# Flagged head programs laid out behind the common one, and head norms as four matmuls side by side

## The chip, the cores and the metric

The kernel runs on one core of one Trainium2 chip. The metric is the device time of one launch in microseconds, taken from its start to its end on the chip. The kernel before took 3060.61 us, the median of 3 runs (3059.5 to 3063.14).

## The reference, cut to what matters

The input X has shape (4, 2048, 256). Four blocks are added to it in turn, each on a layer norm of what came before:

```
x = x + attention_a(layernorm(x))    # 16 heads of 16 channels, causal softmax(q k / 4) v, output projection
x = x + ffn(layernorm(x))            # shift by one token, sigmoid(xr W_r) * (relu(xk W_k)^2 W_v)
x = x + attention_b(layernorm(x))    # decayed keys of unit length times exp(10 key_scale), shifted queries,
                                     # mixed values of unit length, causal softmax, output projection
x = x + ffn(layernorm(x))            # the same feed-forward weights
```

Softmax in the kernel takes no row maximum where the scores of a head can't be large. Whether they can is found on the chip: a head is *flagged* when a bound on its scores is over 64. For attention A the bound is the largest query norm times the largest key norm of the head over all 2048 tokens of a batch, and for attention B the square of the key scale. In this case no head of A is flagged, and one head of the 16 of B is, for each of the four batches.

## The kernel before, in words

**Instances and slots.** The eight attentions (A and B of four batches, the list `ATT`) have four groups of four heads each, which makes 32 *instances*, n = 0 to 31. An instance is 68 *slots* of scores and products (`GROUPS`, `SETS`). For each slot TensorE makes scores with four 32-column tiles at once (`scores`, `matmul` at L863), ScalarE takes the exponential of 128x1024 of them (L819), GpSimd masks the diagonal (L722), and TensorE multiplies the probabilities with the values, four heads in four column tiles (`products`, L1070). Scores are made three slots ahead (`AHEAD`), in three pairs of PSUM banks; VectorE takes the sums out (`take`, L1430 and on).

**Jobs.** Projections, layer norms and feed-forward parts are *jobs* of 512 tokens, whose parts are put at slots by tables written by hand: `T_P` for the projections of attention A (kind P, 16 jobs), `T_M`, `T_B` and `T_END` for the rest. Each part takes one PSUM bank, whose place in the rotation is computed by `number_parts`. Each engine walks through the same slots and at each slot does its share of every job (`interleaved`, and on TensorE `slots`). P jobs of the first batch run ahead of instance 0; those of the second run in instances 0 to 3, and the others in 12, 13, 14, 15 and 16 to 19 at slots that follow the tables.

**Head norms.** A P job makes queries and keys for 512 tokens. VectorE squares their bf16 high parts (L1229), and TensorE sums the squares over the 16 channels of each head: two parts, `n0` for queries and `n1` for keys, each of two matmuls with 16 columns that add up in a 16x512 result (L918). VectorE takes the maximum of each part (`n_max`, L1234). After the fourth job of a batch VectorE takes the maximum of the four, multiplies queries' and keys' and compares (L1240 to L1244), TensorE turns the column of 16 flags to a row (the part `flag`, L925), and VectorE writes flags and the four group flags as integers (L1250 to L1255, semaphore `s_fl`).

**Branches on TensorE.** At the start of an instance TensorE loads the group's flag into a register (L1098) and branches (L1101). The stream of instructions holds the *plain* program of the instance, then its *flagged* program, then the `joined` block with the next load. The plain program first raises two semaphores for VectorE, whose flagged code waits on them (L1103 and the next line), runs its 68 slots, and jumps over the flagged program to `joined` (L1108); 12 slots ahead of the jump stands a prefetch hint (L1106). The flagged program goes through the four heads with a load and an If each (L1005, L1006); for a flagged head `row_maxima` makes all its scores once more in 40 matmuls and 16 for the mask (L990, L993), VectorE takes the maxima (L1388), TensorE turns them (L997), and SyncE places them by DMA in three rows of the queries (`place_maxima`, semaphore `placed`). Then come the 68 slots with the mask added by TensorE, and `joined` follows without a jump. The flagged instances here are 11, 15, 27 and 31, each with its fourth head (j = 3). VectorE and SyncE have Ifs of their own in their streams.

## Time and profile before

| | |
|---|---|
| median of 3 runs | 3060.61 us |
| the profiled execution's own time | 3063.15 us |
| its span, from the first to the last instruction | 3060.4 us |
| TensorE matmul busy | 2873.7 us (94%), 42980 matmuls |
| ScalarE busy | 2234.9 us (73%) |
| VectorE busy | 1482.4 us (48%) |
| GpSimd busy | 818.8 us (27%) |
| mean granted TensorE clock | 0.970 |

The profiled execution took 2.75 us more than its span. Busy time is the union of the spans of an engine's instructions; loads of weights are counted apart from matmuls. Branches, register loads and semaphore instructions are not counted as busy; a wait of an engine that ends with nothing that the profile shows to have released it is called "issue".

### The profile page before, as it was taken

The page shows a single profiled execution, that of the slowest core. Times are in us where ns is not written, and L with a number is a line of the kernel's source. Part 1 is how long each engine was busy: PE and PEld are TensorE (multiplying, and loading weights), DVE is VectorE, ACT ScalarE, POOL GpSimd, SP SyncE. Part 2 cuts the span into 40 slices and gives each one's busy share as a digit, 9 for nine tenths or more (in the row PEclk, how much of TensorE's full clock was granted, in tenths as well). Part 3 has the DMA queues.
Part 4 walks back from the last instruction along what each step waited for, and adds up shares of the span by engine and source line. Part 5 has one row for each costly group of instructions (what it writes and reads, how often), then busy time and mean ns, then how long its engine had stood idle before and what let it go on. Part 6 is the DMA issues. An engine that isn't in the chain of part 4 may idle for free.

```text
span 3060.4 us, 99660 instructions
## 1 busy us (share of the span) xinstructions
PE 2873.7 (94%) x42980; PEld 1286.8 (42%) x42980; DVE 1482.4 (48%) x3566; ACT 2234.9 (73%) x2487; POOL 818.8 (27%) x1246
## 2 busy tenths in 40 slices
PE   6999999999999799997999999999999979999697
PEld 3444444444444344443544444444444424444243
DVE  5322345565555664444344434555566555433344
ACT  2799877787787377883778877778778747888372
POOL 3222223333333222221222222333333312322011
PEclk9999999999999799997999999999999979999798
DMA  5332222222322123221322233222222211222111
GB/s 135 102 85 77 86 59 77 70 72 68 84 73 63 38 70 107 87 67 56 91 78 74 84 91 88 65 81 70 71 60 80 69 51 51 79 70 82 35 61 39
DMA packets 229839, 225.61 MB, mean 74 GB/s; under 512 B 33221, under 2 KB 212933, under 8 KB 229320
## 3 DMA queue, kind: packets, MB, share of 16 engines
q1 hardware_dynamic: 228504, 217.47, 25.0%
q8 instruction: 379, 6.21, 0.9%
q14 instruction: 140, 1.15, 0.1%
q10 hardware_dynamic: 816, 0.79, 0.1%
HBM read 146.80 MB, written 71.32 MB: 71 GB/s over the span
## 4 chain that ended last, share of the span: by engine, by line
PE 73%; DVE 15%; issue 7%; ACT 4%; POOL 1%; DMA 0%; SPq 0%; DVEq 0%; ACTq 0%
PE ps L863 46%; PE ps L1070 23%; ACT probs L819 3%; DVE pmax L1388 3%; PE ps L875 2%; DVE xn L1156 2%; DVE nw_y L1138 1%; DVE nw_u L1136 1%; DVE ln_st L1144 1%; DVE nw_u L1134 1%; DVE k_blk L1367 1%; DVE x_buf L1269 1%; DVE o_blk L1430 1%; DVE nw_v L1343 0%; POOL buf_k L694 0%
## 5 line engine op out<-in xcount | busy, mean ns | idle before, releaser
L819 ACT ACTIVATE probs<-ps 128x1024 f32<-128x1024 f32 x2176 | 2085.7, 1058 | 528.2 <-PE ps L863 525.0
L863 PE MATMUL ps<-q_st,k_st 99*32 99x256 bf16 (+3 forms) x20480 | 1247.8, 349 | 40.4 <-issue 20.8
L1070 PE MATMUL ps<-probs,v_st 128*17 128x512 f32 (+3 forms) x10240 | 1166.5, 532 | 15.5 <-POOL probs L722 9.0
L863 PEld LDWEIGHTS ps<-q_st,k_st 99*32 99x32 bf16 x20480 | 556.9, 96 | 815.7 <-issue 457.1
L722 POOL TENSOR_SCALAR_AFFINE_SELECT probs<-probs 128x256 f32<-128x256 f32 (+1 forms) x896 | 435.9, 503 | 1199.8 <-ACT probs L819 1187.8
L1070 PEld LDWEIGHTS ps<-probs,v_st 128*17 128x17 f32 x10240 | 290.1, 98 | 268.7 <-issue 57.8
L863 PE MATMUL ps<-xT,wT 128*32 128x512 f32 x2048 | 244.7, 594 | 0.0
L1430 DVE STREAM_TRANSPOSE o_blk<-ps 128x512 f32<-128x512 f32 x128 | 91.0, 711 | 273.3 <-PE ps L1070 273.0
L648 POOL TENSOR_TENSOR parts<-rest,parts 128x512 bf16<-128x512 f32 x96 | 120.9, 1259 | 318.3 <-DVE parts L1179 318.3
L1302 DVE SCALAR_TENSOR_TENSOR buf_v<-buf_v,ps 128x512 f32<-128x512 f32 x64 | 44.0, 688 | 273.1 <-PE ps L863 273.1
L1269 DVE TENSOR_TENSOR x_buf<-x_buf,ps 128x512 f32<-128x512 f32 x64 | 43.8, 685 | 235.3 <-PE ps L863 230.6
L863 PE MATMUL ps<-buf_k,wT 128*32 128x512 f32 x1024 | 125.3, 612 | 8.1 <-DVE buf_k L1289 8.1
L863 PE MATMUL ps<-wT,o_in 128*32 128x256 f32 x2048 | 127.3, 387 | 5.4 <-issue 5.2
L863 PEld LDWEIGHTS ps<-xT,wT 128*32 128x32 f32 x2048 | 66.4, 109 | 137.6 <-issue 133.4
L863 PE MATMUL ps<-wT,buf_u 128*32 128x256 f32 x2048 | 121.8, 379 | 1.6 <-issue 1.6
L863 PE MATMUL ps<-wT,buf_a 128*32 128x256 f32 x2048 | 121.5, 379 | 0.6 <-issue 0.5
L990 PE MATMUL ps<-k_st,q_st 99*128 99x512 bf16 (+3 forms) x160 | 66.7, 532 | 57.6 <-issue 51.3
L875 PE MATMUL ps<-ident,xn 128*128 128x128 f32 x512 | 85.0, 291 | 33.7 <-DVE xn L1156 19.7
L1174 DVE TENSOR_TENSOR rest<-ps,parts 128x512 f32<-128x512 f32 x64 | 44.2, 690 | 134.1 <-ACT parts L769 134.1
L783 ACT ACTIVATE buf_u<-ps 128x512 f32<-128x512 f32 x64 | 38.2, 597 | 96.8 <-PE ps L863 96.8
L875 PEld LDWEIGHTS ps<-ident,xn 128*128 128x128 f32 x512 | 55.1, 143 | 123.3 <-DVE xn L1156 63.3
L1388 DVE TENSOR_REDUCE pmax<-ps 128x1 f32<-128x1024 f32 (+4 forms) x96 | 80.4, 905 | 47.8 <-PE ps L993 47.7
(137 smaller groups left out, 2153.1 us busy)
## 6 DMA issues: line engine op xcount, KB each, us to landing
part_a<-parts SPq DMA_DIRECT2D x192, 128.0 KB
x_buf<-in_L_attn_a_X SPq DMA_DIRECT2D x32, 512.0 KB, 4.7
q_st<-part_a SPq DMA_DIRECT2D x128, 128.0 KB
o_chan<-o_out SPq DMA_DIRECT2D x64, 256.0 KB, 2.5
o_in<-o_chan SPq DMA_DIRECT2D x64, 256.0 KB, 4.5
q_st<-part_b SPq DMA_DIRECT2D x128, 128.0 KB
k_st<-part_a SPq DMA_DIRECT2D x64, 192.0 KB, 3.0
part_b<-parts SPq DMA_DIRECT2D x96, 128.0 KB
```

Source lines behind the costliest of these rows:

```text
L648: pool.tensor_tensor(parts[:, u % NPARTS, 2, :], rest[:, u % 2, :], parts[:, u % NPARTS, 1, :], ALU.subtract).then_inc(s_low, 1)
L722: last = pool.affine_select(out=o, in_=o, compare_op=ALU.is_ge, fill=0.0, base=0, pattern=[[0, o.shape[1]], [1, P]], channel_multiplier=-1)
L819: nc.scalar.activation(probs[:, g % NP_BUF, :], ps[:, bk:bk + 2, :].rearrange("p a n -> p (a n)"), ACT.Exp, scale=SCALE[ATT[g // (NHG * NG ...
L863: last = pe.matmul(o[c:c + 32], kt[:, c:c + 32], q, **how)
L875: last = pe.transpose(ps[:, part.bank, tb * P:(tb + 1) * P], src[:, tb, kt * P:(kt + 1) * P], ident[:, :])
L990: last = pe.matmul(o[:, 0:w], qq[:, qb * P:(qb + 1) * P], kk[:, bk * CH:bk * CH + w], start=True, stop=True)
L1070: last = pe.matmul(ps[32 * j:32 * j + VW, bank, q0:q0 + w], v_st[:, k % 2, kb, hg * HG + j, :], p, start=(kb == 0), stop=(kb >= TB * qc), ...
L1156: last = nc.vector.tensor_scalar(xn[:, tb, :], x[:, tb, :], ln_mv[:, tb, 0:1], nw_y[:, tb:tb + 1], ALU.subtract, ALU.mult)
L1174: nc.vector.tensor_tensor(left, src, high, ALU.subtract).then_inc(s_side[part.bank], 1)
L1269: nc.vector.tensor_tensor(half(x, i), half(x, i), ps[:, part.bank, :], ALU.add).then_inc(s_side[part.bank], 1)
L1388: nc.vector.tensor_reduce(pmax[:, 1 if b0 else 0, qb:qb + 1], src, AX_X, ALU.max).then_inc(s_mx["used"], 1)
L1430: nc.vector.transpose(o_blk[:, sg % 2, :], ps[:, 6 + sg % 2, :]).then_inc(s_o, 1)
```

## The change

The flagged programs of all 32 instances are laid out behind the whole common program. The plain program of an instance follows directly on its branch, and the next instance's load follows directly on the plain program; the jump over, its hint and the two semaphore raises go. VectorE raises the two semaphores itself, in the branches of its own in which it skips. A flagged program is now: five short blocks `check0` to `check4`, four blocks `rows0` to `rows3`, each of which jumps back to the next check, and `masked` with the 68 slots, which jumps back to the common program, with a prefetch hint 12 slots ahead. The common program ends with a jump over all flagged ones.

For the head norms a P job now has one part `n`: four matmuls with one 128x32 selector, each into column tile i of one bank, for queries and keys of both halves of the channels. The maximum is taken over 128 partitions in one instruction, the column of 128 maxima is turned by TensorE, and the product and the comparison are made on the row.

```diff
 
-T_P = {"load": -10, "ln": 0, "t0": 8, "t1": 12, "u0": 14, "u1": 16, "u2": 18, "u3": 20, "v0": 22, "v1": 24, "n0": 27,
-       "n1": 29, "flag": 32, "store": 4}
-T_P0 = {"load": -10, "ln": 0, "t0": 6, "t1": 8, "u0": 14, "u1": 16, "u2": 18, "u3": 20, "v0": 22, "v1": 24, "n0": 27,
-        "n1": 29, "flag": 32, "store": 4}
-T_P1 = {"load": -10, "ln": 0, "t0": 8, "t1": 10, "u0": 13, "u1": 18, "u2": 20, "u3": 22, "v0": 24, "v1": 26, "n0": 29,
-        "n1": 31, "flag": 33, "store": 4}
+T_P = {"load": -10, "ln": 0, "t0": 8, "t1": 12, "u0": 14, "u1": 16, "u2": 18, "u3": 20, "v0": 22, "v1": 24, "n": 28,
+       "flag": 31, "store": 4}
+T_P0 = {"load": -10, "ln": 0, "t0": 6, "t1": 8, "u0": 14, "u1": 16, "u2": 18, "u3": 20, "v0": 22, "v1": 24, "n": 28,
+        "flag": 31, "store": 4}
+T_P1 = {"load": -10, "ln": 0, "t0": 8, "t1": 10, "u0": 13, "u1": 18, "u2": 20, "u3": 22, "v0": 24, "v1": 26, "n": 30,
+        "flag": 33, "store": 4}
 T_M = {"load": -10, "o0": 0, "o1": 2, "ln": 3, "t0": 12, "t1": 14, "diff": 13, "shift": 16, "k0": 18, "k1": 20, "r0": 26,
        "r1": 28, "f0": 30, "f1": 32, "out": 34}
...
         ident = sb("ident", [P, P])
         ident_b = sb("ident_b", [P, P], BF16)
...
-        n_top = sb("n_top", [H, 2])
-        fl_prod = sb("fl_prod", [H, 1])
-        fl_col = sb("fl_col", [H, 1])
+        n_max = sb("n_max", [P, NCH])
+        n_top = sb("n_top", [P, 1])
+        fl_row = sb("fl_row", [1, P])
+        fl_prod = sb("fl_prod", [1, H])
         fl_any = sb("fl_any", [1, NHG])
...
@@ -907,22 +907,21 @@
                 for i in range(2):
                     if at == j.off[f"v{i}"]:
                         project_tokens(j.at[f"v{i}"], WV, i, src)
-                for side in range(2):
-                    if at == j.off[f"n{side}"]:
-                        part = j.at[f"n{side}"]
-                        if j is JOBS[0]:
-                            pe.wait_ge(s_const, 2)
-                        pe.wait_ge(s_sq, 4 * (j.at["p"] + 1))
-                        free_bank(part)
-                        for kt in range(KT):
-                            last = pe.matmul(ps[0:H, part.bank, :], head_sel[:, kt, :], squares[:, 2 * kt + side, :],
-                                             start=(kt == 0), stop=(kt == KT - 1))
-                        last.then_inc(s_part, 1)
+                if at == j.off["n"]:
+                    part = j.at["n"]
+                    if j is JOBS[0]:
+                        pe.wait_ge(s_const, 2)
+                    pe.wait_ge(s_sq, 4 * (j.at["p"] + 1))
+                    free_bank(part)
+                    for i in range(4):
+                        last = pe.matmul(ps[32 * i:32 * (i + 1), part.bank, :], head_sel[:, :],
+                                         squares[:, 2 * (i % 2) + i // 2, :], start=True, stop=True)
+                    last.then_inc(s_part, 1)
-                    pe.matmul(ps[0:1, part.bank, 0:H], fl_col[:, :], ident[0:H, 0:H], start=True,
+                    pe.matmul(ps[0:1, part.bank, 0:P], n_top[:, :], ident[:, :], start=True,
                               stop=True).then_inc(s_part, 1)
...
-            def maxima(n):
-                if n:
-                    pe.wait_ge(s_probs, n * NG)
+            def flagged(n):
+
+                def body(what):
+                    return nc.body(f"heads{n}_{what}", parent=from_start, valid_engines=[mybir.EngineType.PE])
+
                 k, hg = divmod(n, NHG)
                 for j in range(HG):
-                    flag = pe.value_load(flags_of(k)[:, hg * HG + j:hg * HG + j + 1])
-                    with pe.If(flag > 0):
+                    with body(f"check{j}"):
+                        if j == 0 and n:
+                            pe.wait_ge(s_probs, n * NG)
+                        flag = pe.value_load(flags_of(k)[:, hg * HG + j:hg * HG + j + 1])
+                        pe.br_cond(flag == 0, f"heads{n}_check{j + 1}", f"heads{n}_rows{j}")
+                with body(f"check{HG}"):
+                    pe.br(f"heads{n}_masked")
+                for j in range(HG):
+                    with body(f"rows{j}"):
                         row_maxima(n, j)
-                    with pe.Else():
-                        pe.sem_inc(s_mx["scores"], NMP)
-                        pe.sem_inc(s_mx["turned"], 1)
-                pe.wait_ge(s_mx["placed"], 48 * HG * (n + 1))
+                        pe.br(f"heads{n}_check{j + 1}")
+                with body("masked"):
+                    end = (n + 1) * NG - AHEAD
+                    pe.wait_ge(s_mx["placed"], 48 * HG * (n + 1))
+                    slots(n * NG - AHEAD, end - HINT_AHEAD, True)
+                    back = pe.mark_branch_hint_location()
+                    slots(end - HINT_AHEAD, end, True)
+                    pe.br(f"joined{n}").branch_hint(back)
...
+            from_start = nc.cur_bb
             for n in range(NI):
...
-                plain, flagged, joined = (f"heads{n}_{what}" for what in ("plain", "flagged", "joined"))
-                end = (n + 1) * NG - AHEAD
-                pe.br_cond(any_flag == 0, plain, flagged)
-                with nc.body(plain, valid_engines=[mybir.EngineType.PE]):
-                    pe.sem_inc(s_mx["scores"], NMP * HG)
-                    pe.sem_inc(s_mx["turned"], HG)
-                    slots(n * NG - AHEAD, end - HINT_AHEAD, False)
-                    over_flagged = pe.mark_branch_hint_location()
-                    slots(end - HINT_AHEAD, end, False)
-                    pe.br(joined).branch_hint(over_flagged)
-                with nc.body(flagged, valid_engines=[mybir.EngineType.PE]):
-                    maxima(n)
-                    slots(n * NG - AHEAD, end, True)
-                    pe.br(joined)
-                nc.switch_bb(joined)
+                pe.br_cond(any_flag == 0, f"heads{n}_plain", f"heads{n}_check0")
+                nc.switch_bb(f"heads{n}_plain", parent=from_start)
+                slots(n * NG - AHEAD, (n + 1) * NG - AHEAD, False)
+                nc.switch_bb(f"joined{n}", parent=from_start)
             slots(NTOT - AHEAD, LAST_SLOT, False)
+            pe.br("heads_done")
+            for n in range(NI):
+                flagged(n)
+            nc.switch_bb("heads_done", parent=from_start)
...
-                for side in range(2):
-                    yield j.t0 + j.off[f"n{side}"]
-                    part = j.at[f"n{side}"]
-                    dve.wait_ge(s_part, part.n + 1)
-                    nc.vector.tensor_reduce(n_max[:, side, j.c:j.c + 1], ps[0:H, part.bank, :], AX_X,
-                                            ALU.max).then_inc(s_side[part.bank], 1)
+                yield j.t0 + j.off["n"]
+                part = j.at["n"]
+                dve.wait_ge(s_part, part.n + 1)
+                nc.vector.tensor_reduce(n_max[:, j.c:j.c + 1], ps[:, part.bank, :], AX_X,
+                                        ALU.max).then_inc(s_side[part.bank], 1)
                 if j.c < NCH - 1:
                     return
-                for side in range(2):
-                    dve.wait_ge(*emptied(j.at[f"n{side}"]))
-                step(nc.vector.tensor_reduce(n_top[:, :], n_max[:, :, :], AX_X, ALU.max))
-                settle()
-                step(nc.vector.tensor_tensor(fl_prod[:, :], n_top[:, 0:1], n_top[:, 1:2], ALU.mult))
-                settle()
-                nc.vector.tensor_scalar(fl_col[:, :], fl_prod[:, :], 1.1 * SCALE["A"] ** 2, SAFE * SAFE, ALU.mult,
-                                        ALU.is_gt).then_inc(s_flc, 1)
+                dve.wait_ge(*emptied(part))
+                nc.vector.tensor_reduce(n_top[:, :], n_max[:, :], AX_X, ALU.max).then_inc(s_flc, 1)
                 yield j.t0 + j.off["flag"]
                 part = j.at["flag"]
                 dve.wait_ge(s_part, part.n + 1)
+                nc.vector.tensor_copy(fl_row[:, :], ps[0:1, part.bank, 0:P]).then_inc(s_side[part.bank], 1)
+                dve.wait_ge(*emptied(part))
+                tops = fl_row[:, :].rearrange("o (s k e) -> o s k e", s=2, k=KT)
+                prod = fl_prod[:, :].rearrange("o (k e) -> o k e", k=KT)
+                step(nc.vector.tensor_tensor(prod, tops[:, 0, :, 0:H // KT], tops[:, 1, :, 0:H // KT], ALU.mult))
+                settle()
+                step(nc.vector.tensor_scalar(fl_prod[:, :], fl_prod[:, :], 1.1 * SCALE["A"] ** 2, SAFE * SAFE, ALU.mult,
+                                             ALU.is_gt))
+                settle()
                 fl = flags["A"][:, j.b % 2, :]
-                step(nc.vector.tensor_copy(fl[:, 0:H], ps[0:1, part.bank, 0:H]))
-                nc.vector.tensor_reduce(fl_any[:, :], ps[0:1, part.bank, 0:H].rearrange("o (g j) -> o g j", j=HG), AX_X,
-                                        ALU.max).then_inc(s_side[part.bank], 1)
-                dve.wait_ge(*emptied(part))
+                step(nc.vector.tensor_copy(fl[:, 0:H], fl_prod[:, :]))
+                step(nc.vector.tensor_reduce(fl_any[:, :], fl_prod[:, :].rearrange("o (g j) -> o g j", j=HG), AX_X,
+                                             ALU.max))
                 settle()
                 nc.vector.tensor_copy(fl[:, H:H + NHG], fl_any[:, :]).then_inc(s_fl, 1)
...
                         with dve.If(flag > 0):
                             row_maxima(n, j)
                         with dve.Else():
+                            dve.sem_inc(s_mx["scores"], NMP)
+                            dve.sem_inc(s_mx["turned"], 1)
                             dve.sem_inc(s_mx["used"], NMP)
                             dve.sem_inc(s_mx["col"], 1)
                             dve.sem_inc(s_mx["step"], 3)
                             dve.sem_inc(s_mx["row"], 1)
                 with dve.Else():
+                    dve.sem_inc(s_mx["scores"], NMP * HG)
+                    dve.sem_inc(s_mx["turned"], HG)
                     dve.sem_inc(s_mx["used"], NMP * HG)
                     dve.sem_inc(s_mx["col"], HG)
                     dve.sem_inc(s_mx["step"], 3 * HG)
```

## Rows read from the trace of the kernel before

**Rows 1.** The page's part 4: the chain that ended last, by engine.

```profile
PE 73%; DVE 15%; issue 7%; ACT 4%; POOL 1%; DMA 0%; SPq 0%; DVEq 0%; ACTq 0%
```

**Rows 2.** Groups of instructions: count | busy us, mean ns | idle before, releaser.

```profile
L819 ACT ACTIVATE probs<-ps 128x1024 f32<-128x1024 f32 x2176 | 2085.7, 1058 | 528.2 <-PE ps L863 525.0
```

**Rows 3.** Line L1108: whole span, then its first and last long one, ns.

```profile
L1108 PEldq COMPARE_BRANCH  x28: 305/416/3277, 165.5 to 2862.3; - x28
...
L1108 PEldq COMPARE_BRANCH  x1: 3042/3042/3042, 312.1 to 312.1; - x1
...
L1108 PEldq COMPARE_BRANCH  x1: 3277/3277/3277, 2862.3 to 2862.3; - x1
```

**Rows 4.** The timeline of ScalarE: start us, us, line, count, idle before.

```profile
235.08 7.75 ACT L819 ACTIVATE probs<-ps 128x1024 f32<-128x1024 f32 x8
...
317.22 1.94 ACT L819 ACTIVATE probs<-ps 128x1024 f32<-128x1024 f32 x2 [2.89 <-PE ps L863]
320.15 2.86 ACT L819 ACTIVATE probs<-ps 128x1024 f32<-128x1024 f32 x3 [0.99 <-PE ps L863]
...
1968.21 1.94 ACT L819 ACTIVATE probs<-ps 128x1024 f32<-128x1024 f32 x2 [1.40 <-PE ps L863]
...
2053.66 1.94 ACT L819 ACTIVATE probs<-ps 128x1024 f32<-128x1024 f32 x2 [1.26 <-PE ps L863]
...
2140.21 1.94 ACT L819 ACTIVATE probs<-ps 128x1024 f32<-128x1024 f32 x2 [1.25 <-PE ps L863]
...
2228.38 1.94 ACT L819 ACTIVATE probs<-ps 128x1024 f32<-128x1024 f32 x2 [3.22 <-PE ps L863]
...
2315.91 1.94 ACT L819 ACTIVATE probs<-ps 128x1024 f32<-128x1024 f32 x2 [3.00 <-PE ps L863]
...
2698.72 1.94 ACT L819 ACTIVATE probs<-ps 128x1024 f32<-128x1024 f32 x2 [3.84 <-PE ps L863]
```

**Rows 5.** The windows: busy us of each engine, granted clock, DMA.

```profile
316.10:319.40 3.30, 3.27 (x32) 1.40 (x36) 0.00 (x0) 1.94 (x2) 0.58 (x2) 0.50 0.51 152
```

**Rows 6.** Line L1101, at 1395.7, then whole span: min/median/max ns.

```profile
L1101 PEldq COMPARE_BRANCH  x1: 4712/4712/4712, 1395.7 to 1395.7; - x1
...
L1101 PEldq COMPARE_BRANCH  x32: 63/71/5130, 92.8 to 2866.0; - x32
```

**Rows 7.** Line L1006 in three windows of instance 11: min/median/max ns.

```profile
L1006 PEldq COMPARE_BRANCH  x1: 2915/2915/2915, 1009.2 to 1009.2; - x1
...
L1006 PEldq COMPARE_BRANCH  x1: 1608/1608/1608, 1013.8 to 1013.8; - x1
...
L1006 PEldq COMPARE_BRANCH  x1: 179/179/179, 1038.7 to 1038.7; - x1
```

**Rows 8.** The timeline of TensorE in instance 11.

```profile
1016.34 0.27 PE L990 MATMUL ps<-k_st,q_st 99*128 99x128 bf16 x1 [11.98 <-issue]
...
1041.82 0.62 PE L863 MATMUL ps<-q_st,k_st 99*32 99x512 bf16 x4 [4.30 <-DMA q_st<-m_part]
```

**Rows 9.** The timeline of TensorE around a head norm of instance 0.

```profile
135.90 0.38 PE L918 MATMUL ps<-buf_a,head_sel 128*16 128x512 bf16 x1
...
136.12 0.38 PE L918 MATMUL ps<-buf_a,head_sel 128*16 128x512 bf16 x1
```

**Rows 10.** The timeline of ScalarE around the same head norm.

```profile
136.99 1.94 ACT L819 ACTIVATE probs<-ps 128x1024 f32<-128x1024 f32 x2 [0.19 <-PE ps L863]
139.16 4.69 ACT L819 ACTIVATE probs<-ps 128x1024 f32<-128x1024 f32 x5 [0.23 <-PE ps L863]
```

**Rows 11.** Timelines ahead of instance 0: TensorE, then VectorE.

```profile
52.94 0.83 PE L875 MATMUL ps<-ident,xn 128*128 128x128 f32 x4 [2.87 <-DVE n_max L1234]
...
89.10 1.28 DVE L1234 TENSOR_REDUCE n_max<-ps 16x1 f32<-16x512 f32 x2 [1.73 <-PE ps L918]
```

**Rows 12.** The timeline of the end.

```profile
3051.83 3.62 PE L863 MATMUL ps<-wT,buf_u 128*32 128x256 f32 x64
...
3056.97 0.39 SPq L456 DMA_DIRECT2D out<-x_buf  x1
```

21 lines of the change are left out of this document (10 added, 11 removed).

## The prediction

> **What bounds the kernel now.** I read the page first. TensorE has matmuls in flight for 94% of the span (the table above) and holds 73% of the chain that ended last [rows 1]. ScalarE is the second: its 2176 exponentials take 2085.7 us, and of its 528.2 us of idle time before them 525.0 end with TensorE's scores [rows 2]. So a microsecond in which TensorE issues nothing costs about one, unless ScalarE has scores in hand or a job's VectorE work ends later anyway. Second I asked what "issue" is, 7% of the chain [rows 1], by the lines with branches. TensorE jumps over a flagged program 28 times. The jump takes 0.31 us at best and 0.42 in the median, but up to 3.28 [rows 3]; looked at one by one, 16 take at most 0.5 us, two 0.9, and ten over 2.0 (the first 3.04 at 312.1, the last 3.28 at 2862.3 [rows 3]), though each has its prefetch hint. Third, ScalarE's timeline shows what such a jump costs. At 240 it goes from instance to instance without a break; after the 3.04 us jump it is idle 2.89 and then 0.99 us more [rows 4], the second since TensorE was granted 0.50 of its clock, its lower level of 1.2 GHz, from 316.1 to 319.4, after it had stood still [rows 5]. Fourth come the four flagged instances. The branch into one takes 4.71 to 5.13 us [rows 6], skips over unflagged heads 2.92 and 1.61 [rows 7], and from the last common matmul to the first of the row maxima TensorE is idle 11.98 us [rows 8].
>
> **Plain boundaries (gain 24.5 us).** The jump and its hint go, and the next program follows in line. What stays is the register load and the untaken branch, which takes 0.06 or 0.07 us now [rows 6]. By jump: (a) into instance 3: the idle 2.89 + 0.99 = 3.9. (b) Into 5, 6, 7, 24, 25 and 26 part of the wait lies beside VectorE's norm and residual chain. I therefore take whole instances of like jobs: with short jumps at both ends 2053.66 - 1968.21 = 85.45 and 2140.21 - 2053.66 = 86.55, mean 86.0; with a long one at the end 2228.38 - 2140.21 = 88.17 and 2315.91 - 2228.38 = 87.53, mean 87.85 [rows 4]. A long jump costs 1.8, and six 10.8. (c) Into 20: as these, 1.8. (d) Into 29: ScalarE idles 3.84 against 1.25 to 1.40 after short jumps [rows 4], 2.5, and it is followed by the lower clock too, 1.0: 3.5. (e) Ahead of flagged 31 the whole 3.28 less a branch of 0.37 with its load: 2.9. (f) The two of 0.9: 0.5 each. (g) Into 1 and 2, where no job gives cover, 0.3 each; the other short jumps lie under queued matmuls, 0. Sum 3.9 + 10.8 + 1.8 + 3.5 + 2.9 + 1.0 + 0.6 = 24.5. Bounds: 15, if VectorE's chains hold back half of (b) to (d) and the low clock comes elsewhere; 28, if every excess over 0.31 is paid out in full.
>
> **Flagged instances (gain 2.4 us, very uncertain).** Per instance:
> - Way in. Now 12.6 us from the branch to the first score (1003.7 to 1016.3). After it the branch is again taken and its target far. The 5 us came just behind a jump with its own fetch; a branch alone costs what the long jumps show, 2.1 to 3.3: I take 2.7. Four loads and compares with three pairs of semaphore raises are what is left of the 12.6 now: 12.6 - 5.0 - 2.9 - 1.6 = 3.1. The raises go; at an estimated 0.3 a pair, 2.2 stay. The last compare branches over three `rows` bodies, each 40 + 16 + 1 matmuls with as many weight loads, 342 instructions. The skips that missed took 1.6 and 2.9 [rows 7]; I take 2.9. Sum 7.8, gain 4.8. Bounds 0.2 (both jumps at 5.1) and 8.1 (2.1 and 0.2).
> - Way on. Now a branch of 0.18 us at 1038.7 [rows 7], then the wait for the DMA of the maxima until 1041.82 [rows 8], 3.1 us in all. After it TensorE goes back to `check4` and forward over all four bodies to `masked`. Two misses are 2.7 and, since the block behind `check4` is being fetched too, 3.5; with the two short blocks 6.5, beside a DMA of 3.1: loss 3.4. Bounds 0 (both found) and 7.3 (both at 5.1).
> - Way out. The fall into the next block becomes a hinted jump: ten long ones in 28 give 0.8. Bounds 0 and 4.5 (a long one and the lower clock).
>
> Four times (-4.8 + 3.4 + 0.8) = -2.4; bounds -32 and +46. Behind the waiting TensorE nothing else is held up but ScalarE, whose buffers are empty.
>
> Of two statements of the Trainium skill one speaks for, one against the losses on the way on (Runtime: NRT & Kernel Launch, section on instruction fetch mechanics). First the row: a skip ahead over one such body, 114 matmuls and loads, right after a far branch took 2.92 us [rows 7]. The page says that a taken branch whose target isn't in the current two-block window stalls for a DMA; by that, both moves of the way on miss. It gives TensorE at the same time a store of 2048 instructions; by that, `check4` and `masked` would still be there, and the way on would cost nothing. The rival "found" below is worked out by its own rows.
>
> **Head norms (gain 8.6 us).** The two matmuls of a part start 0.215 us apart (135.90, 136.12), both in column tile 0, while the other three tiles go on to the next scores [rows 9]. Four per job are 0.86 us of tile 0; in four tiles they are 0.22. ScalarE's starts 136.99 and 139.16 stand 2.17 us apart for two exponentials, and the pair before it 2.13; without waits five take 4.69, start to end, so they follow 0.92 apart [rows 10]. Norms cost it 2.17 + 2.13 - 4 x 0.92 = 0.6 there, of which some 0.1 stays: 0.55 for each of 12 jobs beside attention, 6.6. Bounds 0 (ScalarE bound anyway) and 7.7. Ahead of instance 0 the maximum of `n1` stands between VectorE's layer norm and the PSUM bank of the next transposes: TensorE waits for it, 2.87 us at 52.94 with the norm, of which the maximum is 0.6, twice [rows 11]. At 89.10 two maxima take 1.28 [rows 11]; one less saves 0.64, norms in parallel 0.4, and the flag row, with one VectorE step more and a wider turn, gives 0.4 back. With 0.2 of shorter matmuls: 1.2 + 0.6 + 0.2 = 2.0. Bounds 0 and 3. The maximum over 128 partitions instead of 16 is put at the same 0.64, as the 512 elements of one partition set it. Later flags are due long before use, and their longer chain is hidden.
>
> **The rest.** VectorE raises two more semaphores at 28 boundaries; TensorE's own took 0.05 us each. Where VectorE's chain is late (about seven instances) this counts: 0.5, bounds 0 and 2. The final jump over all flagged programs comes after TensorE's last matmuls (3055.45), and the output's DMA, issued at 3056.97, ends the kernel near 3060 [rows 12]: even 3.3 us are hidden; without that cover it would cost 3.3. The selector's setup is of the same size, 0.
>
> **Sum.** 24.5 + 2.4 + 8.6 - 0.5 = 35.0. The profiled execution took 3063.15 us (span 3060.4 and 2.75 around it): 3028.1 after. The median of the runs is 2.5 lower, so 3025.6.
>
> **Rivals.**
> - *Found*: backward jumps find their target. For it: nothing was jumped back to in this trace. Against: the forward skips missed. The way on then costs nothing and the way out 0.3, together 3.9 less per instance: 4 x 3.9 = 15.6, and 3010.
> - *Covered*: the waits removed at boundaries are mostly given back to VectorE's chain and to ScalarE. For it: after short jumps ScalarE's first idle is 1.3, but a wait for VectorE follows in such instances. Against: the whole-instance lengths already include that. Plain boundaries give 12, norms 5, flagged 0: 3060.6 - 16.5 = 3044.
> - *Slower by far jumps*: every move of the flagged path (in, to `rows3`, back, to `masked`, out) costs the 5.1 us that the branch in costs now, since each also starts a fetch of the block behind. Then each flagged instance loses 7.3 + 4.5 - 0.2 = 11.6 us, 46 in all, against gains of 32.6: 3074. It decides from a loss of 8.2 us per flagged instance on. For it: 4.7 to 5.1 four times out of four [rows 6]. Against: lone misses are 2.1 to 3.3 [rows 3].
> - *Not as it says*: the straight stream stalls at the boundaries all the same, since some long jumps were fetches that the stream needs anyway. Only norms gain: 3052.
>
> **How the numbers follow.** Forecast 0.60, found 0.12, covered 0.16, slower 0.04, not as it says 0.08. The runs of this kernel lie within 0.12%, so about 0.2%, 6.1 us, can be told from no change: faster means under 3054.5. Faster holds in the forecast, found and covered and in half of the last: 0.92; same 0.04; slower 0.04. The unknown costs around 3025.6 are mainly the flagged path's: a third of its bounds' reach is -10 and +16. The range takes in the found and covered cases: 3007 to 3046.
>
> **What would show it.** No branch of TensorE over 0.1 us at plain boundaries, and ScalarE's break at 317 gone with its low clock. Instances 5 to 7 and 24 to 26 near 86 us. In each flagged instance 7 to 8 us from the branch to the first score of the row maxima, and some 6 instead of 3.1 from the last row maximum to the scores. Norm matmuls starting within 0.05 us of each other, and ScalarE's two starts around them 1.9 apart. The forecast is wrong if flagged instances lose over 5 us each, or if boundaries show a new wait for VectorE as long as the jump was.

## The result and the profile after

The changed kernel takes 3020.3 us, the median of 4 runs (3018.95 to 3021.45), beside 3061.88 us for the kernel before on the same chip (4 runs, 3059.5 to 3064.81). The ratio is 0.9864, with a 95% interval of 0.9847 to 0.9881: 41.6 us are gone, where 35.0 were forecast. The profiled execution's span fell from 3060.4 to 3019.5 us.

First the chain and ScalarE's main group, from the page of the kernel after. They answer to [rows 1, 2]: "issue" has one point less of the chain, and ScalarE's idle time ahead of its exponentials fell by 36 us, all of it waits for scores.

```profile
PE 73%; DVE 15%; issue 6%; ACT 4%; POOL 1%; DMA 0%; SPq 0%; DVEq 0%; ACTq 0%
...
L819 ACT ACTIVATE probs<-ps 128x1024 f32<-128x1024 f32 x2176 | 2082.6, 1061 | 491.8 <-PE ps L863 488.6
```

Next TensorE's branches, in ns (min/median/max, first and last start). L1112 is the branch at the start of an instance: ten in a row from instance 1 on, then the one into instance 11, then all. L1010 is a check's branch (the four of instance 11, then the last of instance 15), L1016 the end of a `rows` body, L1023 the way out.

```profile
L1112 PEldq COMPARE_BRANCH  x10: 63/63/63, 164.5 to 902.2; - x10
...
L1112 PEldq COMPARE_BRANCH  x1: 3935/3935/3935, 991.6 to 991.6; - x1
...
L1112 PEldq COMPARE_BRANCH  x32: 63/63/4078, 90.8 to 2829.8; - x32
...
L1010 PEldq COMPARE_BRANCH  x4: 63/72/1177, 996.0 to 997.4; - x4
...
L1010 PEldq COMPARE_BRANCH  x1: 3819/3819/3819, 1386.1 to 1386.1; - x1
...
L1016 PEldq COMPARE_BRANCH  x4: 179/184/190, 1023.7 to 2859.8; - x4
...
L1023 PEldq COMPARE_BRANCH  x4: 413/1382/1677, 1116.2 to 2967.2; - x4
```

The jumps of [rows 3] are gone, and the untaken branch costs what it cost in [rows 6]. In a flagged instance the way in still has a branch of 3.9 us and a last check of 1.2 to 3.8. At the end of the maxima stands the surprise: L1016 takes 0.18 us.

TensorE's timeline of instance 11 answers to [rows 8]: the idle time ahead of the row maxima fell from 11.98 to 6.08 us, and the wait for the maxima's DMA is the same 4.30. But within the row maxima TensorE then stands still for another 2.37 us, up to 1002.27, with nothing that released it. The kernel before has no such stop, and the other three flagged instances have none.

```profile
998.79 0.27 PE L989 MATMUL ps<-k_st,q_st 99*128 99x128 bf16 x1 [6.08 <-issue]
...
1002.27 0.59 PE L989 MATMUL ps<-k_st,q_st 99*128 99x512 bf16 x1 [2.37 <-issue]
...
1026.79 0.62 PE L863 MATMUL ps<-q_st,k_st 99*32 99x512 bf16 x4 [4.30 <-DMA q_st<-m_part]
```

The boundary into instance 3, in ScalarE's timeline and in a window 3.3 us wide (PEclk is the last figure but two): 20 exponentials follow without a break where [rows 4] had 2.89 and 0.99 us of idle time, and the granted clock is 1.00, the level of 2.4 GHz, where [rows 5] had 0.50.

```profile
304.04 18.73 ACT L819 ACTIVATE probs<-ps 128x1024 f32<-128x1024 f32 x20
...
309.30:312.60 3.30, 3.08 (x56) 1.07 (x48) 0.00 (x0) 3.30 (x5) 2.35 (x6) 1.00 0.50 151
```

Around a head norm of instance 0, TensorE first, then ScalarE: four norm matmuls take 0.43 us together, and nine exponentials follow one another where [rows 10] had a gap ahead of and behind a pair.

```profile
135.63 0.43 PE L917 MATMUL ps<-buf_a,head_sel 128*32 128x512 bf16 x4
...
134.15 8.37 ACT L819 ACTIVATE probs<-ps 128x1024 f32<-128x1024 f32 x9 [0.20 <-PE ps L863]
```

One line has no counterpart in the argument ahead of the result. At the boundary into instance 7, VectorE's next operation behind its own branch comes 3.00 us late, with no releaser. GpSimd and, through it, TensorE's products then wait, and ScalarE behind them. Boundaries with such a wait of VectorE, over 0.6 us, are eight in the kernel after (1.7 to 3.4 us) and five in the kernel before (1.6 to 3.8 us), and only the ones into 24 and 28 are in both lists:

```profile
649.01 1.30 DVE L1374 TENSOR_TENSOR k_blk<-k_blk,nw_v 128x1024 f32<-128x1024 f32 x1 [3.00 <-issue]
...
651.13 1.05 PE L1082 MATMUL ps<-probs,v_st 128*17 128x512 f32 x8 [2.13 <-POOL probs L722]
...
652.66 6.52 ACT L819 ACTIVATE probs<-ps 128x1024 f32<-128x1024 f32 x7 [2.07 <-PE ps L863]
```

VectorE jumps over its own flagged code there, without a hint.

### The profile page after: what moved, and what is told of

Its sections match the earlier page's. It is cut to its first block, busy times and chain, and to the rows that moved or that the text cites. A ratio compares the mean times of both kernels' runs of the same rounds, so it can differ in the third digit from the quotient of the medians.

```text
span 3019.5 us, 99577 instructions
## 1 busy us (share of the span) xinstructions
PE 2861.9 (95%) x42980; PEld 1297.9 (43%) x42980; DVE 1468.2 (49%) x3554; ACT 2231.9 (74%) x2487; POOL 814.7 (27%) x1246
## 4 chain that ended last, share of the span: by engine, by line
PE 73%; DVE 15%; issue 6%; ACT 4%; POOL 1%; DMA 0%; SPq 0%; DVEq 0%; ACTq 0%
PE ps L863 46%; PE ps L1082 23%; ACT probs L819 4%; DVE pmax L1395 3%; PE ps L875 3%; DVE xn L1162 2%; DVE nw_y L1144 1%; DVE nw_u L1142 1%; DVE ln_st L1150 1%; DVE nw_u L1140 1%; DVE x_buf L1276 1%; DVE o_blk L1441 1%; POOL probs L722 0%; DVE nw_v L1350 0%; DVE k_blk L1374 0%
## 5 line engine op out<-in xcount | busy, mean ns | idle before, releaser
L863 PE MATMUL ps<-q_st,k_st 99*32 99x512 bf16 (+3 forms) x20480 | 1235.4, 349 | 22.7 <-DMA q_st<-m_part 18.3
L863 PEld LDWEIGHTS ps<-q_st,k_st 99*32 99x32 bf16 x20480 | 563.6, 96 | 794.8 <-issue 448.7
L863 PE MATMUL ps<-wT,o_in 128*32 128x256 f32 x2048 | 126.6, 386 | 14.3 <-issue 14.3
L875 PE MATMUL ps<-ident,xn 128*128 128x128 f32 x512 | 85.7, 292 | 33.8 <-DVE xn L1162 24.5
L672 POOL TENSOR_TENSOR buf_a<-xf 128x512 f32<-128x512 f32 x32 | 33.1, 1035 | 259.0 <-DVE xf L1168 244.2
```

Source lines behind the costliest of these rows:

```text
L863: last = pe.matmul(o[c:c + 32], kt[:, c:c + 32], q, **how)
L875: last = pe.transpose(ps[:, part.bank, tb * P:(tb + 1) * P], src[:, tb, kt * P:(kt + 1) * P], ident[:, :])
```

## The experiments

Times are medians, "before" is the kernel before on the same chip in the same hours (3059.5, 3059.6 and 3056.4 us in the three sets), and a ratio is to it. To see where a difference lies, I took the length of each instance from ScalarE's timeline, from its first exponential to the next instance's. The table gives, in us against the kernel before, the start of instance 0, the ten plain instances with norm jobs (0 to 3, 12, 13, 16 to 19), the fourteen that have none, and the eight that are flagged or end in a flagged one (10, 11, 14, 15, 26, 27, 30, 31). The rest up to the span is the tail.

| kernel | median us | start | 10 with norms | 14 without | 8 flagged | span |
|---|---|---|---|---|---|---|
| after | 3020.3 | -1.7 | -14.8 | -11.5 | -12.6 | -40.9 |
| e1_layout | 3034.2 | +1.1 | -8.3 | -6.6 | -9.9 | -24.5 |
| e2_norms | 3045.5 | -1.4 | -1.4 | -8.2 | -5.3 | -16.7 |
| e3_vector_too | 3001.3 | -2.0 | -14.6 | -25.1 | -18.6 | -61.3 |
| e10_both_layouts | 3013.4 | -0.4 | -9.3 | -24.8 | -15.7 | -51.2 |
| e6_vector_alone | 3049.2 | +1.6 | -1.7 | -8.9 | -4.4 | -14.3 |
| e7_one_tile | 3030.9 | -0.6 | -8.4 | -7.9 | -12.8 | -29.9 |
| e5_no_hint | 3172.7 | -0.5 | +49.7 | +50.0 | +10.3 | +109.0 |

**The two halves of the change.** e1_layout is the kernel before with the new layout and VectorE's raises, e2_norms the kernel before with the new norms.

```diff
 e1_layout: the blocks of the new layout, with the old norms
-                with nc.body(plain, valid_engines=[mybir.EngineType.PE]):
...
+                nc.switch_bb(f"heads{n}_plain", parent=from_start)
...
 e2_norms: the old layout, with the new norms
-                for side in range(2):
-                    if at == j.off[f"n{side}"]:
...
+                if at == j.off["n"]:
```

> The kernel before with the new order of TensorE's programs alone (and VectorE raising the two semaphores); norms as before. Theory, that the layout gives the most: 41.6 us less 8.6 of norms, 33 below the kernel before, about 3029; no TensorE branch over 0.1 us at plain boundaries, jump from the last row maximum to the masked program not over 0.2 us. Rival, that the forecast of 27 for the layout was right and the norms give 15: 3035.

> The kernel before with the new norms alone, branches and layout as before. Theory, my terms: 12 jobs of 0.55 and 2.0 ahead of instance 0, 8.6 below the kernel before, about 3053; ScalarE's waits around a norm gone. Rival, norms give 15 since ScalarE gets ahead: 3047. Rival, the block boundaries of the instruction stream shift and other jumps are long: anything within 8 us of 3053, which the lengths of the 28 jumps would show.

The layout alone took 25.3 us off (3034.15 us, ratio 0.9921, 0.9907 to 0.9934), the norms alone 14.0 (3045.49 us, 0.996, 0.9946 to 0.9974). Their sum, 39, is the whole change within its uncertainty. The layout came within 1.1 us of its forecast of 26.4, and the 33 us of the theory above did not come. The norms brought 5 more than their 8.6, but not where the norms are: by the table only 2.8 of the 16.7 us of e2_norms lie ahead of instance 0 and in the ten instances with norm jobs, and 8.2 lie in the fourteen without. The rival that other jumps are long holds beside the theory. With the new norms nine of the 28 jumps of TensorE take over 2 us, not the same ten (the ones into 24 and 29 take 0.33 us, where they took 2.29 and 3.13, and the one into 27 takes 2.22 instead of 0.90), and VectorE waits at seven boundaries instead of five. Instance 28 alone is 4.6 us shorter by this and instance 9 3.7, while 4 and 24 are 2.5 and 2.6 longer. So 14.0 us is what this program gained and not the price of its norms.

**VectorE's jumps.** e3_vector_too is the kernel after with VectorE's flagged programs laid out behind its common one as well.

```diff
-                with dve.If(grp > 0):
...
+                dve.br_cond(any_flag == 0, f"vector{n}_plain", f"vector{n}_check0")
+                nc.switch_bb(f"vector{n}_plain", parent=from_start[0])
```

> The changed kernel with VectorE's flagged programs laid out behind its common one as well. In the changed kernel VectorE's first instruction after its branch comes 2.7 to 3.1 us late at five plain boundaries (0.45 at the others), and behind three of them TensorE waits 2.1 us for masked probabilities. Theory, that these are fetches of code after VectorE's own jump: no gap over 0.6 us after its branches at plain boundaries, the three waits gone with the low clock after one of them, 6 to 10 us less than 3020.3, so 3010 to 3014. Rival, that the waits belong to GpSimd's order of work: gaps gone, time within 3 us of 3020.

It took 3001.26 us (0.9816, 0.9802 to 0.9829), 19 less than the kernel after, where 6 to 10 were expected. VectorE's timeline at the boundary into instance 7 shows the 3.00 us gone:

```profile
644.50 1.32 DVE L1375 TENSOR_TENSOR k_blk<-k_blk,nw_v 128x1024 f32<-128x1024 f32 x1 [0.26 <-DVE ln_st L1151]
```

The table says where it came from: 13.6 us in the fourteen instances without norm jobs, 6 in the flagged eight, none in the ten. So 19 us of the kernel after were VectorE's waits. e6_vector_alone made the same edit on the kernel before.

> The kernel before, with VectorE's flagged programs laid out behind its common one, and TensorE as it was. With TensorE's flagged programs already behind and the norms in four tiles, the same edit on VectorE took 19 us off. Theory A (VectorE's late work after its own jumps is a wait of its own place, at other boundaries than TensorE's): it takes 10 to 19 us off here too, 3042 to 3050 us. Theory B (it counts only once TensorE's jumps are gone, since both engines jump at the same boundary and the one hides the other): it takes 0 to 5 us off, 3055 us or more. In the trace VectorE has no idle time over 0.6 us behind its branches either way, and TensorE still has ten or so jumps over 2 us.

It took 3049.19 us (0.9966, 0.9954 to 0.9978), 10.4 less: the low end of theory A. About half of the 19 us counts beside TensorE's jumps, the other half only once these are gone. This is what the rival "covered" foresaw in kind, but it took a third of what there was to gain, not half: TensorE's layout is worth 25.3 us beside VectorE's jumps and 35.8 without them (3049.2 - 3013.4, the next run).

**Norms with and without those waits.** e10_both_layouts has both engines' layouts and the old norms.

> The flagged programs of TensorE and of VectorE both laid out behind the common ones, head norms as before. It stands to the kernel with both layouts and the new norms (3001.3 us) as the layout of TensorE alone (3034.2) stands to the kernel after (3020.3): there the norms were worth 14 to 16 us, of which, instance by instance, 8.5 lie in the instances that have norms and 2.8 ahead of the first, and 5 in instances that have none. Theory (those 5 us are VectorE's own jumps, whose long waits fall on other boundaries when the length of its program changes): with those jumps gone the norms are worth 11 us, 3012 us. Rival (a real effect of the norms on what follows): 14 to 16 us, 3015 to 3018 us. And the layout of VectorE alone is worth 20 us or more beside the old norms.

It took 3013.42 us (0.9845, 0.9831 to 0.9858). With VectorE's jumps gone the norms are worth 3013.4 - 3001.3 = 12.1 us, as the theory had it. Of the 10.1 us between the two spans, 5.2 lie in the ten instances with norm jobs (0.60 to 0.73 in eight of them, 0.38 in instance 12, and instance 0 is 0.3 longer), 1.6 ahead of instance 0, and 2.9 in the flagged eight, of which 14 and 15 have a norm job each.

**Tiles or parts.** e7_one_tile keeps one part and one maximum but puts all four matmuls into column tile 0.

```diff
-                        last = pe.matmul(ps[32 * i:32 * (i + 1), part.bank, :], head_sel[:, :],
+                        last = pe.matmul(ps[0:32, part.bank, :], head_sel[:, :],
```

> The kernel after, with all four norm matmuls of a part in column tile 0 of the bank; the norms of three of the four groups of rows are left out of the maximum by that, which moves no time. One part, one maximum and the place in the rotation stay. Theory (the norms cost since they stand one behind the other in one tile): 0.86 us of tile 0 per part as before, 12 parts beside attention give back 0.5 us each and the prologue 0.4 x 4 at most: 6 to 8 us slower than after, 3026 to 3028 us, and ScalarE's two starts around a norm again 1.2 us apart instead of 0.9. Rival (the second part, its bank and its maximum were what cost): within 2 us of after, 3020 to 3022 us.

It took 3030.91 us (0.9898, 0.9883 to 0.9913), 10.6 more than the kernel after. The rival is out: the ten instances with norm jobs give back 0.5 to 0.8 us each, and ScalarE's gap around the norm is there again, in its timeline:

```profile
135.12 4.03 ACT L819 ACTIVATE probs<-ps 128x1024 f32<-128x1024 f32 x4 [0.20 <-PE ps L863]
139.42 5.61 ACT L819 ACTIVATE probs<-ps 128x1024 f32<-128x1024 f32 x6 [0.27 <-PE ps L863]
```

It was 3 us over the expectation, and the instances tell why: 7, 21 and 24 have no norm job and yet are 1.3 to 1.5 us longer, to 89.49, 89.44 and 89.23 us. e1_layout has 89.49 and 89.57 in 7 and 24. At the boundary into 7, TensorE waits the same 2.13 us as in the kernel after. What differs is the clock behind it. TensorE's timeline, ScalarE's, and a window of e7_one_tile:

```profile
654.63 1.88 PE L1082 MATMUL ps<-probs,v_st 128*17 128x512 f32 x8 [2.13 <-POOL probs L722]
...
657.40 1.94 ACT L819 ACTIVATE probs<-ps 128x1024 f32<-128x1024 f32 x2 [3.31 <-PE ps L863]
...
654.80:658.10 3.30, 3.30 (x28) 1.24 (x24) 3.02 (x14) 0.69 (x1) 0.59 (x2) 0.50 0.22 69
```

And windows of the kernel after, first right behind its wait, which ends at 651.13, then at the boundary into 10, where the same wait of 2.13 us was followed by the lower level:

```profile
651.20:654.50 3.30, 3.30 (x56) 1.73 (x59) 3.02 (x14) 1.84 (x3) 0.68 (x2) 1.00 0.25 74
...
913.40:916.70 3.30, 3.30 (x39) 1.73 (x32) 2.92 (x16) 1.94 (x2) 0.00 (x0) 0.50 0.22 82
```

So a stop of 2.1 us is sometimes followed by 3.3 us at 1.2 GHz, which costs another 1.5 us in the instance, and sometimes not. The three instances make 4.2 of the 10.6 us, and what is left, 6.4, is what the theory named. They don't come from the one tile: e4_back_jump, below, has the norms in four tiles and the same three at 89.50, 89.55 and 89.09 us. Between e1_layout and the kernel after, two of them, 7 and 24, make 3.1 of the norms' 14, and instance 20, where a wait of VectorE of 3.92 us is no longer there, 1.9 more: luck of place, not a saving of the norms. What decides whether the clock falls I did not settle.

**What the hint was worth.** e5_no_hint is the kernel before without the prefetch hint of the 28 jumps.

```diff
-                    over_flagged = pe.mark_branch_hint_location()
...
-                    pe.br(joined).branch_hint(over_flagged)
+                    pe.br(joined)
```

> The kernel before, with the prefetch hint of TensorE's 28 jumps over a flagged program left out; nothing else differs. Theory (a jump costs the fetch of its target, and a hint mostly hides it): the 18 jumps that take 0.3 to 0.9 us with the hint take 2 to 3.3 us without, each of them costs the 1.8 us that a long one cost in the instances of like jobs, 18 x 1.8 = 32, and the kernel takes some 3090 us. Rival A (the ten long jumps are the only ones that need a fetch at all, hint or not): 3060 us and the same ten long jumps. Rival B (the jumps wait mostly beside VectorE and ScalarE work): all 28 long, but under 3072 us.

It took 3172.68 us (1.0367, 1.0351 to 1.0383), 113 more. Neither rival holds, and the theory's price was too low. The 28 jumps take 117.8 us together instead of 33.1, and TensorE is at the lower clock level for 302 us of the span instead of 187. Line L1107 is the jump; behind the one into 5, ScalarE's timeline has two gaps, the second again at the lower clock:

```profile
L1107 PEldq COMPARE_BRANCH  x28: 3247/4190/5324, 165.1 to 2970.6; - x28
...
506.14 1.94 ACT L819 ACTIVATE probs<-ps 128x1024 f32<-128x1024 f32 x2 [6.68 <-PE ps L863]
511.76 3.77 ACT L819 ACTIVATE probs<-ps 128x1024 f32<-128x1024 f32 x4 [3.68 <-PE ps L863]
```

An unhinted jump takes 3.2 to 5.3 us, 4.2 in the median. That the ten "long" jumps of the kernel before, 2.0 to 3.3 [rows 3], were hinted fetches not yet done fits this, but no run with an earlier hint shows it. The branch into a flagged instance, which never had a hint, belongs to this row and not to those: it takes 3.4 to 4.1 us in the kernel after. One unhinted jump over code never run does not fit. The last one of the kernel after, over all flagged programs (L1117), took 0.31 us; the same jump took 0.30 to 0.32 us in seven other versions with the new layout and 3.61 in e8_rows_last. Why stays open.

**Jumping back.** e4_back_jump has the wait for the maxima in `check4` instead of `masked`, so that this block is no longer empty. e8_rows_last lays `masked` right behind the checks and the `rows` bodies behind it.

```diff
 e4_back_jump
                 with body(f"check{HG}"):
+                    pe.wait_ge(s_mx["placed"], 48 * HG * (n + 1))
                     pe.br(f"heads{n}_masked")
...
                 with body("masked"):
...
-                    pe.wait_ge(s_mx["placed"], 48 * HG * (n + 1))
 e8_rows_last
                 with body(f"check{HG}"):
                     pe.br(f"heads{n}_masked")
+                with body("masked"):
+                    ...
                 for j in range(HG):
                     with body(f"rows{j}"):
...
```

> The changed kernel with the wait for the placed maxima moved from the masked program into the last check block, so that this block holds an instruction and TensorE has to go back to it and forward again. My forecast's price for the two jumps was 6.5 us beside a DMA of 3.1, a loss of 3.4 per flagged instance, 14 in all: 3034. Rival, that jumps back find their target: 3020. Rival, 5.1 us each: 7.3 per instance, 3049.

> The kernel after, with `masked` laid out directly behind the checks and the four `rows` bodies behind it. The last check now branches over `masked` and three bodies to `rows3`, and from `rows3` TensorE goes back over all of them. In the kernel after, the way on took 0.18 us for the jump and 3.1 us of waiting for the maxima's DMA, and nothing more. Theory (there the target of the jump stood right behind it, so that nothing had to be fetched; a jump back costs as much as an unhinted jump forward, 3.3 to 5.3 us in the kernel without hints, and the DMA covers 3.1): the way on takes 3.3 to 5.5 us from the jump to the first score, the last check's branch 2.5 to 4.5 us instead of 1.2 to 3.8, and the kernel takes 3022 to 3034 us. Rival (programs already passed through stay at hand): the way on 3.1 to 3.3 us as before, 3019 to 3025 us.

e4_back_jump took 3021.72 us (0.9884, 0.9869 to 0.99): no price that stands clear of the noise, since by its span it is 1.8 us faster than the kernel after and by the ratios 6 us slower, with intervals that overlap. Its profile has what the kernel after lacks, the branch of `check4` itself, and it takes 0.18 us. Here `masked`, four bodies ahead of the check, was reached without a stall; it lies right behind `rows3`, so that it may have come in with that body, and this run doesn't tell whether a target never near would have. In the kernel after no branch of the empty `check4` is recorded, and the way on is one jump of 0.18 us to the code right behind. e8_rows_last took 3026.9 us (0.9905, 0.9887 to 0.9923). By its span it is 3.3 us slower than the kernel after, by the medians 6.6, by the ratios 12. The rival on the way on is right; the theory's price for the last check's branch is right too. Line L1013 of e4_back_jump is `check4`'s branch:

```profile
L1013 PEldq COMPARE_BRANCH  x4: 174/177/180, 1024.2 to 2862.7; - x4
```

L1023 of e8_rows_last is the jump back over `masked` and three bodies, and TensorE's timeline has the same wait for the DMA behind it as the kernel after:

```profile
L1023 PEldq COMPARE_BRANCH  x4: 190/192/194, 1025.1 to 2863.3; - x4
...
1028.16 0.62 PE L863 MATMUL ps<-q_st,k_st 99*32 99x512 bf16 x4 [4.30 <-DMA q_st<-m_part]
```

What it loses lies on the way in, whose last branch takes 3.5 to 4.0 us, all four times, where the kernel after has 1.2 to 3.8.

**The way in.** On e3_vector_too as base, e9_near_rows lays the flagged head's body first, and e11_hint_in adds a hint for the branch into the flagged program, whether it is taken or not.

```diff
 e9_near_rows
-                for j in range(HG):
+                for j in reversed(range(HG)):
                     with body(f"rows{j}"):
 e11_hint_in, besides
-                pe.br_cond(any_flag == 0, f"heads{n}_plain", f"heads{n}_check0")
+                away = pe.br_cond(any_flag > 0, f"heads{n}_check0", f"heads{n}_plain")
+                if n:
+                    away.branch_hint(ahead)
...
+                ahead = pe.mark_branch_hint_location()
```

> The kernel with both engines' flagged programs behind (3001.3 us), with TensorE's `rows` bodies in the order 3, 2, 1, 0, so that the flagged head's body stands right behind the checks, and `masked` three bodies further. Theory (the last check's branch, 1.2 to 3.8 us and 2.2 in the mean, is the fetch of a target three bodies away, and that of the way on is hidden beside the maxima's DMA of 3.1 us): the branch takes 0.1 to 0.3 us, or up to 1 where the straight stream itself waits for its fetch; 4 x 2 = 8 us gained less what the way on gives back, 0 to 1.5 each: 2989 to 2998 us. Rival (the time is that of a fetch which the code needs anyway, near or far, and comes back as a stall within the row maxima): 2999 to 3002 us.

> The kernel with both layouts and the `rows` bodies in the order 3, 2, 1, 0; TensorE's branch at an instance's start is now taken when a head is flagged, and it has a prefetch hint of its target 12 slots ahead, on all instances but the first, whether it will be taken or not. Theory (the branch in takes 3.4 to 4.1 us since nothing has fetched its target, and a fetch that isn't used costs the common path nothing, as it is followed by what comes next in line): the branch in takes 0.2 to 2.5 us, 1.5 to 3.5 us gained in each of four flagged instances, 6 to 14 us under the same kernel without the hint. Rival (the hinted block takes the place of the one that comes next in line): 27 plain boundaries get a stall of some 2 us each, of which half is covered, 25 us slower or more. A third case: both, and the sum near nothing.

e9_near_rows took 3000.05 us (0.9818, 0.9804 to 0.9832), the same as its base. The last check's branch did fall to 0.24 us, and TensorE reached the row maxima 1.2 to 3.5 us sooner after its branch in, but two of four jumps on the way on now take 3.3 and 3.4, and VectorE isn't ready. Line L1010 at 1375.1, L1016, and TensorE's timeline:

```profile
L1010 PEldq COMPARE_BRANCH  x1: 239/239/239, 1375.1 to 1375.1; - x1
...
L1016 PEldq COMPARE_BRANCH  x4: 318/1798/3445, 1012.9 to 2840.6; - x4
...
991.41 0.61 PE L989 MATMUL ps<-k_st,q_st 99*128 99x512 bf16 x1 [3.59 <-DVE pmax L1396]
```

e11_hint_in took 3013.18 us (0.9861, 0.9845 to 0.9876), 13 more than e9_near_rows: the rival in kind, at half its size. Eleven of the 32 instances are 0.5 to 4.5 us longer than in e9_near_rows, not all that have the unused hint. The hint works, 0.40 us for the branch into instance 11, and brings nothing. TensorE is at the maxima by 987.6 and waits 8.00 us for VectorE, which after its own branch is idle for 6.53 (TensorE's and VectorE's timelines). At plain boundaries the unused hint costs: ScalarE waits 2.31 and 3.69 us behind the first exponential of instance 14, where e9_near_rows has one wait of 1.52; the lower clock level, from 1293.5 to 1296.9 us, is in this too.

```profile
L1112 PEldq COMPARE_BRANCH  x1: 401/401/401, 984.9 to 984.9; - x1
...
996.30 0.61 PE L989 MATMUL ps<-k_st,q_st 99*128 99x512 bf16 x1 [8.00 <-DVE pmax L1401]
...
995.95 16.68 DVE L1401 TENSOR_REDUCE pmax<-ps 128x1 f32<-128x128 f32 x21 [6.53 <-issue]
...
1292.77 1.02 ACT L819 ACTIVATE probs<-ps 128x1024 f32<-128x1024 f32 x1 [2.31 <-PE ps L863]
1297.48 2.86 ACT L819 ACTIVATE probs<-ps 128x1024 f32<-128x1024 f32 x3 [3.69 <-PE ps L863]
```

The best version is the kernel after with VectorE's flagged programs behind as well: 3001.3 us, or 3000.1 with the nearer body.

## Why the prediction was right, and where it was not

**What bounds.** Right: time in which TensorE issues nothing was worth about its length, and the 36 us that ScalarE no longer waits are most of the 40.9.

**Plain boundaries, 24.5.** The branches did as said, 0.063 us each, and (a) is exact, with its clock. The bound of 28, "if every excess over 0.31 is paid out in full", is mis-summed: the 28 jumps take 33.1 us, so their whole excess is 24.5, the forecast itself. The step that failed stands in the rival "covered", that the lengths 85.45 to 88.17 us [rows 4] "already include" what VectorE takes back. They hold the waits that VectorE had in the kernel before, and not those that it has once TensorE's layout is changed. VectorE had waits of its own at these boundaries, of 1.6 us at the one into 24 from which the price was taken and 3.7 at the one into 5, and with the new layout they fell on others and were more: eight, of 3.0 to 4.4 us, in e1_layout. Its timeline in the kernel before, which the argument had not looked at:

```profile
486.01 1.23 DVE L1367 TENSOR_TENSOR k_blk<-k_blk,nw_v 128x1024 f32<-128x1024 f32 x1 [3.71 <-issue]
...
2231.00 1.86 DVE L1367 TENSOR_TENSOR k_blk<-k_blk,nw_v 128x1024 f32<-128x1024 f32 x1 [1.64 <-issue]
```

Instances 5 and 6 came to 86.17 and 86.76 us, near the 86 forecast, but 7, 21 and 24 to 88.0. In the 24 plain instances e1_layout gained 14.9 us. With VectorE's jumps gone too, the same instances gained 34.1 (e10_both_layouts), of which VectorE's own layout makes 10.7 (e6_vector_alone). The difference, 23.4 us, is what TensorE's jumps cost there when VectorE has none, beside a forecast of 21.6: the price of 1.8 for a long jump was about right, and VectorE's waits took back 8.5 us that the sum had at nothing. The argument had looked at TensorE's branch lines alone.

**Flagged instances, 2.4.** The eight instances gained 9.9 us in e1_layout, of which 2.9 had been forecast at the boundary ahead of 31 as (e). The way in was right in sum and not in its terms. From the branch to the first score it takes 7.2, 10.0, 7.7 and 7.6 us, mean 8.1, where 7.8 was forecast; but the branch takes 3.4 to 4.1 instead of 2.7, the price of the unhinted row, and the checks less than put. The way on is wrong: "back to `check4` and forward to `masked`" as two misses, +3.4 each. It costs nothing, since the empty block is skipped, and e4_back_jump and e8_rows_last show that neither a second move nor a jump back is a fetch here. This was the rival "found", which had 0.12. Four times 3.4 is 13.6 us, the largest error of the sum. In e1_layout 4.6 of it show (9.9 against 5.3); with VectorE's jumps gone on both sides 6.0 do (15.7 less the 4.4 of e6_vector_alone is 11.3). The way in and the way out take back 2.8 more than forecast, and the rest isn't accounted for. The way out took 0.4 to 1.7, mean 1.2, against 0.8.

Of the two statements of the Trainium skill weighed there (Runtime: NRT & Kernel Launch, instruction fetch mechanics) the trace agrees with TensorE's store of 2048 instructions on the way on: L1023 of e8_rows_last, 0.19 us, goes back to code right behind the checks, which ran 26 to 29 us before, with one `rows` body run in between. It does not agree with a window of two blocks there. Where code had not been run through, forward, unhinted, the stall that the page names appeared 28 times out of 28 (L1107, 3.2 us or more), and at the last jump of the new layout, L1117, it did not.

**Head norms, 8.6.** Right in mechanism, and in size where the terms can be read one by one. Of the terms, 0.55 per job beside attention is 0.60 to 0.73 in most instances, and the prologue's 2.0 is 1.6 (e10_both_layouts against e3_vector_too). The ten and the two in 14 and 15 add up to 6.3 us; with the prologue 7.9 of 10.1 are explained, and the last 2 lie in flagged instances and are not. Where VectorE still jumps the norms brought 14, beside either layout. Between e1_layout and the kernel after, 4.9 us of the difference lie in the fourteen instances without norms, of which 3.1 are low-clock stretches that did not occur and 1.9 VectorE's wait in instance 20; in e2_norms 8.2 do. This part is luck of place, and the forecast had no term for it.

**The rest and the end.** The raises on VectorE can't be told from its other waits. The final jump took 0.3 us ahead of the output's DMA, where even 3.3 had been called hidden.

**The signs named.** TensorE's branches at plain boundaries, the break at 317 and its clock, and the norm matmuls (at most 0.04 us apart) came as named. The 6 us on the way on did not: it is 3.1 as before. And one sign of being wrong did come, "a new wait for VectorE as long as the jump was": 3.00 us into instance 7, where the jump had taken 2.2. That the time was near all the same is in part luck.

The sum was low by 6.6 us, of which the norms are 5.4. The close hit of the layout, 25.3 for 26.4, is two errors that nearly cancel: 6.7 too much at plain boundaries (14.9 against 21.6, the 24.5 without (e)) and 4.6 too little in the flagged instances. Behind them stand larger ones: a way on that was charged 13.6 us and costs nothing, and 8.5 us of VectorE's waits that no term held.

## What to carry to other kernels

A jump over code that never ran cost some 4 us here unhinted and, for one in three hinted ones, still 2 to 3: lay rare code behind the common stream on every engine that has it, since the engine left over takes back part of the gain. When a price is taken from lengths of whole stages, look first whether another engine has the same event at the same place, and whether its waits stay where they were when the program changes. A gain measured between two programs belongs to the edit only as far as it lies where the edit acts. A shorter way in on one engine is worth only what the slowest engine of that way allows.

## What the runs showed that was not expected

- An unhinted jump over one flagged program took TensorE 3.2 to 5.3 us; with the hint 18 of 28 took under 1 us.
- The one jump over all 32 flagged programs, at the end, took 0.31 us, without a hint.
- TensorE jumped back over `masked` and three `rows` bodies in 0.19 us, without a stall.
- A hint whose branch isn't taken is not free: with it the kernel took 11 us more by the spans and 13 by the medians.
- A wait of 2.13 us on TensorE was followed by 3.3 us at the lower clock level in one case and not in another, in otherwise like instances, and the low stretch made the instance 1.5 us longer.
